# A gated cross-attention and expert layer on one Trainium2 core: the last norm's root on two engines, the clip flag in registers, the heads in another order

## The reference

```python
x = x + tanh(g_xattn[0]) * xattn(layernorm(x), ctx_768, Wq, bq, Wk, bk, Wv, bv, Wo, bo)
x = x + tanh(g_ffn[0]) * ffn(layernorm(x), gate_weight, w1, b1, w2, b2)
# layernorm: (x - mean) / sqrt(var + 1e-5), over the last axis
# xattn: 8 batches, 512 queries of width 256, 512 keys of width 192, 16 heads of 16
attn = clip(q @ k.T * 16 ** -0.5, -10000, 10000)
attn = softmax(attn)
attn = where(any(isnan(attn)), 1 / 512, attn)
out = (attn @ v) @ Wo + bo
# ffn: 8 experts of 1024 hidden units over all 4096 tokens
logits = x @ gate_weight.T
gates = logits * (logits >= the 6144th smallest logit)
y = sum over experts e of gates[:, e] * (gelu(x @ w1[e].T + b1[e]) @ w2[e].T + b2[e])
```

## Time and profile before

| | us |
|---|---|
| three executions | 1980.11, 1981.48, 1983.56 (median 1981.48) |
| profiled execution | 1980.04 |
| its span | 1978.2 |
| TensorE busy | 1891.1 (96%) |
| VectorE busy | 1323.6 (67%) |
| ScalarE busy | 1241.2 (63%) |
| GpSimd busy | 147.0 (7%) |
| TensorE's granted clock over the span | 0.979 of full |

### The profile page before, as it was taken

One profiled execution on the slowest core, in us unless ns is written; L12 is line 12 of the kernel. 1 busy time (PEld: TensorE's weight loads), 2 busy tenths in 40 slices (PEclk: granted clock), 3 DMA queues, 4 the chain that ended last, 5 costly groups with the idle time before them and its releaser, 6 DMA issues.

```text
span 1978.2 us, 26040 instructions
## 1 busy us (share of the span) xinstructions
PE 1891.1 (96%) x8916; PEld 1356.8 (69%) x8916; DVE 1323.6 (67%) x2331; ACT 1241.2 (63%) x2081; POOL 147.0 (7%) x330
## 2 busy tenths in 40 slices
PE   6989999999968999999999999999999999999998
PEld 5743333333336877788788888878878888887886
DVE  6688888888734798565655665565665566656555
ACT  4447776776742323676766766667676676767665
POOL 4300111101112250000000000000000000000000
PEclk9979999999978999999999999999999999999999
DMA  7943323222110154433323333223422224232221
GB/s 239 332 124 87 87 69 83 72 72 73 50 54 24 75 187 178 154 117 112 107 85 123 144 116 108 86 107 128 144 92 106 107 91 164 102 112 85 107 107 54
DMA packets 97243, 220.81 MB, mean 112 GB/s; under 512 B 31314, under 2 KB 49492, under 8 KB 87892
## 3 DMA queue, kind: packets, MB, share of 16 engines
q1 hardware_dynamic: 97108, 219.12, 32.4%
HBM read 178.57 MB, written 40.24 MB: 111 GB/s over the span
## 4 chain that ended last, share of the span: by engine, by line
PE 66%; DVE 2%; ACT 1%; issue 1%; POOL 0%; ACTq 0%; DVEq 0%; POOLq 0%
PE ps_y L2152 31%; PE ps_h L2099 27%; PE ps_h L2059 4%; PE ps_y L2071 4%; DVE h_hi L2410 0%; ACT gelu L2313 0%; DVE h_lo L2414 0%; DVE early L2554 0%; DVE gated L2483 0%; DVE out_T_acc L2490 0%; ACT h_hi L2316 0%; ACT w_pair L2283 0%; DVE candidate L2452 0%; DVE w_pair L2539 0%; DVE gate L2471 0%
## 5 line engine op out<-in xcount | busy, mean ns | idle before, releaser
L2414 DVE TENSOR_TENSOR h_lo<-gelu,h_hi 128x512 fp32r<-128x512 f32 x512 | 357.3, 702 | 406.3 <-ACT h_hi L2316 405.2
L2099 PE MATMUL ps_h<-x_hi,w_pair 128*128 128x512 f32 x1568 | 566.7, 395 | 1.4 <-ACT gelu L2313 1.0
L2313 ACT ACTIVATE gelu<-early,b 128x512 f32<-128x512 f32 x336 | 243.1, 724 | 228.4 <-DVE early L2554 220.9
L2099 PEld LDWEIGHTS ps_h<-x_hi,w_pair 128*128 128x128 f32 x1568 | 294.5, 188 | 77.1 <-issue 5.5
L964 DVE TENSOR_REDUCE low<-ps_s 128x1 f32<-128x512 f32 x512 | 322.2, 684 | 32.9 <-PE ps_s L820 29.5
L2316 ACT ACTIVATE h_hi<-gelu 128x512 fp32r<-128x512 f32 x448 | 283.3, 632 | 42.0 <-ACT gelu L2313 0.7
L2099 PE MATMUL ps_h<-x_lo,w_pair 128*128 128x512 f32 x784 | 308.8, 394 | 0.0
L1096 ACT ACTIVATE probs_T<-ps_t 128x512 f32<-128x512 f32 x384 | 207.8, 601 | 102.8 <-PE ps_t L830 101.1
L2554 DVE TENSOR_TENSOR early<-ps_h,copy 128x512 f32<-128x512 f32 x336 | 230.5, 686 | 51.1 <-PE ps_h L2099 51.1
L820 PE MATMUL ps_s<-k_st,q_st 48*128 48x512 f32 x512 | 204.0, 477 | 3.2 <-SPq L736 2.0
L2152 PE MATMUL ps_y<-h_hi,w_lo 128*128 128x512 f32 x512 | 203.0, 396 | 0.0
(11 more groups left out here) (252 smaller groups left out, 2611.4 us busy)
## 6 DMA issues: line engine op xcount, KB each, us to landing
x_hi<-blocks_scratch SPq DMA_DIRECT2D x28, 1024.0 KB, 5.1
x_lo<-blocks_scratch SPq DMA_DIRECT2D x28, 1024.0 KB, 8.8
x_hi<-blocks_scratch SPq DMA_DIRECT2D x28, 768.0 KB, 6.8
x_lo<-blocks_scratch SPq DMA_DIRECT2D x28, 768.0 KB, 10.2
gate<-gates_scratch SPq DMA_DIRECT2D x64, 256.0 KB, 3.2
q_st<-q_scratch SPq DMA_DIRECT2D x192, 64.0 KB, 2.4
k_st<-k_scratch SPq DMA_DIRECT2D x192, 64.0 KB, 2.3
k_scratch<-k_hl SPq DMA_DIRECT2D x8, 1024.0 KB, 3.9
```

Source lines behind the costliest of these rows:

```text
L2099: mm = pe.matmul(bank, w[wp], x[xp], start=start and n == 0, stop=n == 2, skip_group_check=not start)
L2313: act.activation(gelu[:, c % GELUS, :], src, ACT.Gelu_apprx_tanh, bias=b1[p][:, j:j + 1]).then_inc(gelu_done, 1)
L2414: dve.tensor_tensor(h_lo[:, j % RING, :], gelu[:, j % GELUS, :], h_hi[:, j % RING, :].bitcast(F32), ALU.subtract).then_inc(h_ready, 1)
```

## The change

Three edits, and bookkeeping for them.

- **Root.** For the last batch alone, GpSimd no longer makes the root. `last_root` on VectorE makes mean and variance, ScalarE takes one square root (`last_deviation`), and VectorE takes the reciprocal and a correction step. ScalarE takes a square root of a zero (`sqrt_ready`) earlier, behind its last weight split.
- **Flag.** Each engine reads the clip flag once, at the end of its list in `build_attend` and behind a semaphore, and keeps it in a register. The three later reads of it go, and the NaN flag's read and test move inside an outer `If(clip > 0)`.
- **Heads.** T takes the heads 0, 2, 1, 3 and S the heads 1, 3, 0, 2. In the first half of a step T has the upper rows and S the lower ones, in the second half the other way round.

```diff
-SCORE_HEADS = (1, 0, 3, 2)
+SCORE_HEADS = (1, 3, 0, 2)
+TURNED_HEADS = (0, 2, 1, 3)
...
+        def load_flag(name, eng):
+
+            eng.wait_ge(fits_summed, 2)
+            keep["clip"][name] = eng.value_load(keep["clip_flag"][0:1, 0:1], min_val=0, max_val=1)
...
-            with pool.Fori(0, BATCH) as b:
-
+            def bias(b):
...
+            with pool.Fori(0, BATCH - 1) as b:
+                bias(b)
                 reciprocal_root(b)
+            bias(BATCH - 1)
+            load_flag("pool", pool)
...
-            def scores_T(b, g, k, j, turn):
-
-                at = (g * TT + k) * GROUP + j
-                if k == 0 and j == 0:
+            def scores_T(b, g, k, i, turn):
+
+                at = (g * TT + k) * GROUP + i
+                j = TURNED_HEADS[i]
+                if k == 0 and i == 0:
...
+            def last_root():
+
+                mean, dev, diff, square, spread, var, root, root_2, scaled, rstd = (moments[:, i, :] for i in range(10))
+                first = (BATCH - 1) * 9
+                dve.wait_ge(stats_done, BATCH * 2)
+                dve.tensor_tensor(diff, stats[:, :, 1], stats[:, :, 4], ALU.subtract)
+                dve.tensor_tensor(dev, stats[:, :, 2], stats[:, :, 5], ALU.add)
+                dve.tensor_tensor(root, stats[:, :, 1], stats[:, :, 4], ALU.add).then_inc(moment_done, 1)
+                dve.wait_ge(moment_done, first + 1)
+                dve.scalar_tensor_tensor(out=square, in0=diff, scalar=0.25, in1=diff, op0=ALU.mult, op1=ALU.mult)
+                dve.tensor_scalar(spread, dev, 1.0 / DIM, EPS, ALU.mult, ALU.add)
+                dve.tensor_scalar(mean, root, 0.5, None, ALU.mult).then_inc(moment_done, 1)
+                dve.wait_ge(moment_done, first + 2)
+                dve.tensor_tensor(var, spread, square, ALU.add).then_inc(moment_done, 1)
+                dve.wait_ge(moment_done, first + 4)
+                dve.reciprocal(root, scaled).then_inc(moment_done, 1)
+                dve.wait_ge(moment_done, first + 5)
+                dve.tensor_tensor(root_2, root, root, ALU.mult).then_inc(moment_done, 1)
+                dve.wait_ge(moment_done, first + 6)
+                dve.scalar_tensor_tensor(out=diff, in0=root_2, scalar=-0.5, in1=var, op0=ALU.mult, op1=ALU.mult).then_inc(moment_done, 1)
+                dve.wait_ge(moment_done, first + 7)
+                dve.scalar_tensor_tensor(out=rstd, in0=diff, scalar=1.5, in1=root, op0=ALU.add, op1=ALU.mult).then_inc(rstd_done, 1)
+
             def layer_norm(b, i):
+                if b == BATCH - 1 and i == 0:
+                    last_root()
...
-                dve.tensor_scalar(keep["clip_flag"][:], ps_t[0][:, 0:1], 3 * HEADS * TOKENS - 0.5, None, ALU.is_lt)
+                dve.tensor_scalar(keep["clip_flag"][:], ps_t[0][:, 0:1], 3 * HEADS * TOKENS - 0.5, None, ALU.is_lt).then_inc(fits_summed, 1)
...
-                for j in heads:
-                    act.wait_ge(t_in_psum, n * GROUP + j + 1)
-                    act.activation(probs_T[k][:, j, :], ps_t[bank_of(turn, (g * TT + k) * GROUP + j)][:], ACT.Exp, scale=-1.0).then_inc(exp_done, 1)
+                for i in places:
+                    act.wait_ge(t_in_psum, n * GROUP + i + 1)
+                    act.activation(probs_T[k][:, TURNED_HEADS[i], :], ps_t[bank_of(turn, (g * TT + k) * GROUP + i)][:], ACT.Exp, scale=-1.0).then_inc(exp_done, 1)
...
+            def last_deviation():
+
+                act.wait_ge(moment_done, (BATCH - 1) * 9 + 3)
+                act.activation(moments[:, 8, :], moments[:, 5, :], ACT.Sqrt).then_inc(moment_done, 1)
...
                         if b == BATCH and (g, k) == (0, TT - 1):
                             first_high(1, w2_raw)
+                            act.activation(sqrt_ready[:], zero[:, 0:1], ACT.Sqrt)
+                        if b == BATCH and (g, k) == (1, TT - 1):
+                            last_deviation()
...
+            load_flag("act", act)
...
-            clip = pe.value_load(keep["clip_flag"][0:1, 0:1], min_val=0, max_val=1)
+            clip = keep["clip"]["pe"]
             with pe.If(clip > 0):
...
-            uniform = pe.value_load(keep["nan_flag"][0:1, 0:1], min_val=0, max_val=1)
-            with pe.If(uniform > 0):
+            clip = keep["clip"]["pe"]
+            with pe.If(clip > 0):
+                uniform = pe.value_load(keep["nan_flag"][0:1, 0:1], min_val=0, max_val=1)
+                with pe.If(uniform > 0):
```

More of the change, by code:

```diff
@@ L1577, in _ @@
         def _(sp):
[L1578 to L1586, removed]
-                    sp.dma_start(x_res[:], io["x"][bass.ds(b * SEQ, SEQ), :].rearrange("(t p) d -> p t d", p=P)).then_inc(batch_loaded, 16)
-                    sp.wait_ge(added, b + 1)
-                    sp.dma_start(scratch["x2"][bass.ds(b * SEQ, SEQ), :].rearrange("(t p) d -> p t d", p=P), x_res[:]).then_inc(x2_stored, 16)
-                batch(0)
-                with sp.Fori(1, BATCH) as b:
-                    batch(b)
-                sp.wait_ge(x2_stored, 16 * BATCH)
+            clip = keep["clip"]["sp"]
@@ new lines, in _, with batch @@
+            with sp.If(clip > 0):
+                uniform = sp.value_load(keep["nan_flag"][0:1, 0:1], min_val=0, max_val=1)
+                with sp.If(uniform > 0):
+                    sp.dma_start(wo[:], io["Wo"].rearrange("(k p) n -> p k n", p=P)).then_inc(consts_ready, 16)
+                    sp.dma_start(bo[:], io["bo"].rearrange("(a n) -> a n", a=1).to_broadcast([P, DIM])).then_inc(consts_ready, 16)
+                    def batch(b):
+                        wait(sp, x2_stored, b * 16)
+                        src = scratch["v"][bass.ds(b, 1), :, :].rearrange("a p (n w) -> (a p) n w", w=VW)
+                        sp.dma_start(v[:].rearrange("p t (h d) -> p (t h) d", d=HDIM), src[:, :, 0:HDIM]).then_inc(batch_loaded, 16)
+                        sp.dma_start(x_res[:], io["x"][bass.ds(b * SEQ, SEQ), :].rearrange("(t p) d -> p t d", p=P)).then_inc(batch_loaded, 16)
+                        sp.wait_ge(added, b + 1)
+                        sp.dma_start(scratch["x2"][bass.ds(b * SEQ, SEQ), :].rearrange("(t p) d -> p t d", p=P), x_res[:]).then_inc(x2_stored, 16)
+                    batch(0)
+                    with sp.Fori(1, BATCH) as b:
+                        batch(b)
+                    sp.wait_ge(x2_stored, 16 * BATCH)
@@ L1596, in _ @@
         @block.gpsimd
         def _(pool):
-            uniform = pool.value_load(keep["nan_flag"][0:1, 0:1], min_val=0, max_val=1)
-            with pool.If(uniform > 0):
-                pool.memset(share[:], 1.0 / SEQ).then_inc(consts_ready, 1)
+            clip = keep["clip"]["pool"]
+            with pool.If(clip > 0):
+                uniform = pool.value_load(keep["nan_flag"][0:1, 0:1], min_val=0, max_val=1)
+                with pool.If(uniform > 0):
+                    pool.memset(share[:], 1.0 / SEQ).then_inc(consts_ready, 1)
@@ new lines, in _ @@
+            with pe.If(clip > 0):
+                uniform = pe.value_load(keep["nan_flag"][0:1, 0:1], min_val=0, max_val=1)
+                with pe.If(uniform > 0):
+                    pe.wait_ge(consts_ready, 33)
+                    with pe.Fori(0, BATCH) as b:
+                        pe.wait_ge(batch_loaded, b * 32 + 32)
+                        for k in range(KT):
+                            for t in range(TT):
+                                mm = pe.matmul(ps_mean[:, k, :], v[:, t, k * P:(k + 1) * P], share[:],
+                                               start=(t == 0), stop=(t == TT - 1))
+                        mm.then_inc(mean_in_psum, 1)
+                        pe.wait_ge(mean_ready, b + 1)
+                        for k in range(KT):
+                            mm = pe.matmul(ps_y[:], mean_T[:, k, :], wo[:, k, :], start=(k == 0), stop=(k == KT - 1))
+                        mm.then_inc(y_in_psum, 1)
@@ L1627, in _ @@
         @block.vector
         def _(dve):
[L1629 to L1640 removed]
+            clip = keep["clip"]["dve"]
@@ new lines, in _ @@
+            with dve.If(clip > 0):
+                uniform = dve.value_load(keep["nan_flag"][0:1, 0:1], min_val=0, max_val=1)
+                with dve.If(uniform > 0):
+                    dve.wait_ge(consts_ready, 33)
+                    with dve.Fori(0, BATCH) as b:
+                        dve.wait_ge(y_in_psum, b + 1)
+                        dve.tensor_tensor(y[:], ps_y[:], bo[:], ALU.add).then_inc(y_ready, 1)
+                        dve.wait_ge(batch_loaded, b * 32 + 32)
+                        dve.wait_ge(y_ready, b + 1)
+                        for t in range(TT):
+                            ins = dve.scalar_tensor_tensor(out=x_res[:, t, :], in0=y[:], scalar=keep["tanh_g"][:, 0:1], in1=x_res[:, t, :],
+                                                           op0=ALU.mult, op1=ALU.add)
+                        ins.then_inc(added, 1)
```

61 lines of the change are left out of this document (22 added, 39 removed).

## The result

The changed kernel takes 1973.49 us (median of 6 runs, 1972.51 to 1975.27), the kernel before, run beside it, 1983.14 (6 runs, 1980.11 to 1985.56). The ratio is 0.9949, 95% interval 0.9938 to 0.9959: faster by 0.51%, or 9.65 us between the medians. Forecast were 3.7. The profiled execution took 1972.75, span 1970.9.

The account below looks back on a forecast made before the run. TensorE was taken as the bound, chiefly in the experts' part, whose earlier start shortens the whole. Root 2.7 + flag 1.5 - heads 0.5 = 3.7 us off the median 1981.48 gave 1977.8 us; range 1974.9 to 1981.0.

Parts of the forecast that it names:

- Root: Last norm's root, between attention and experts: normalising starts 1.84 us behind the statistics instead of 4.61; 2.7 us gained.
- Flag: Clip flag reads at the block ends before the experts: three removed, one added at attention's end; 1.5 us gained.
- Pages: Rival, chance 0.20: experts' code arrives at a fixed time behind the first jump, so the flag gains only 0.2 us.
- Halves: Rival, chance 0.07: in attention, loading weights into a streaming half costs time, 26 us over 120 steps; median 2003.
- Clock behind the root: Rival, chance 0.08: shorter root gap may keep TensorE at 2.4 GHz, some 2.3 us more; 6.0 gained, median 1975.5.
- Last batch: Last two groups of the last batch: lone T pairs share a half; -0.5 us, with 0 and -2.5 as ends.
- Cost in the steady batches 0: Attention's steady batches: the new head order runs the same pairs on two halves, so nothing gained or lost.
- my signs of being wrong: Forecast is wrong if the steady batch moves from 56.0 us, or the root's chain takes over 2.6 us.

Follow-up runs that it names:

- e5: Changed kernel with the old T order 0, 1, 2, 3 in groups 2 and 3 of the last batch: 1974.46 us, ratio 0.9947.
- e1: Kernel before with the two new orders of heads alone, root and flag as before: 1979.80 us, ratio 0.9978.
- e7: Changed kernel with the new head orders only in groups 3 and 0, round the turn of a batch: 1973.15 us, ratio 0.9945.
- e8: Changed kernel with the new head orders only in groups 1 and 2, old ones round the turn: 1979.50 us, ratio 0.9970.
- e9: Changed kernel with the S order made equal to the T order, so each pair needs the same half of TensorE: 2096.73 us, ratio 1.0573.
- e10: Changed kernel with old head orders and one T product computed twice just ahead of each turn and one just behind: 1976.83 us, ratio 0.9965.
- l7: Second profile of the kernel with old head orders and two more T products round each turn; profiled execution 1976.09 us.

## Why the prediction was wrong, point by point

- **Root**: 2.7 forecast, 2.64 measured. The chain took 1.97, 0.13 more than summed: links of 0.20 rather than 0.18, the reciprocal's 0.21. The table load ran at 572.6 and cost nothing.
- **Flag**: 1.5 forecast, 1.44 measured. VectorE's read stands behind the logits, the other engines' earlier.
- **Pages** (0.20): did not occur here. The third jump on TensorE stayed at 0.208.
- **Halves** (0.07, slower): no cost. The batch is 55.97.
- **Clock behind the root** (0.08): no. TensorE's gap was down to 3.07 us (578.60 to 581.67), and its clock still went to 0.50 at 581.9, for 20.5 us.
- **Last batch**: -0.5 forecast, -0.49 measured. That is partly luck, for e5 gave back only 0.24 of it where I had put all.
- **"Cost in the steady batches 0"**: this step failed. It is right of a batch at full clock and wrong of the kernel, for the change took away the stretches of half clock behind the turns, 2.4 to 2.8 us each. Each of the four profiles of before has one, so some 2.6; by whole times e1 measured some 4, and e7 against e8, which differ in the order alone, 6.4 (by their medians). I had that stretch before me in the earlier trace rows, wrote that it comes and goes with the clock, and asked of the new order only what it does to the start of each product. None of my signs of being wrong would have caught it: the full-clock batch stayed at 56.0 and the root's chain under 2.6.

One term is thus missing in the sum, 2.6 by the traces and 4 to 6 by whole times. The time, 1973.49, is 4.3 below the forecast and 1.4 below the range. The gain is 6.0 above the forecast, since the kernel before, too, came out 1.7 above the median that I started from.

**What stays open.** Why the order of the halves acts on the clock; the runs show only that it does, and where. Also, with parts of the change alone the times moved more than the traces account for (root 5.5 by ratio against 2.6; flag 3.2 against 1.3), and the three parts by themselves add up to 0.66% where the whole has 0.51%, and the kernel before's mean of 65, 1984.0, is 2.5 above that of its four profiled executions. None of its profiles is of an execution above 1983, so what those have more is not shown.

## What to carry to other kernels

A batch that is 5% longer than its twins at a granted clock of 0.94 is a row to explain, not to subtract: find where the stretch begins, and ask of each part of a change what TensorE will be doing just there. An order of products that leaves a batch at full clock as long as it was can still be worth as much as the steps that you can add up. And when two profiles differ in such a stretch, count it over several before you believe either.

## What the runs showed that I had not expected

**The clock falls in dense work.** It fell behind a turn after 3 us with TensorE busy 2.79, and in e9 after 3 us with TensorE busy without a gap. The profile's busy columns are no forecast of the granted clock; the windows' PEclk column has to be read by itself.

**What the rival with the pages named, a third jump that grows, came one kernel further.** e10 puts 16 more products into TensorE's code, and TensorE's jump over the clipped version of the experts' block grew. That line in e10:

```profile
L2079 PEldq COMPARE_BRANCH  x1: 1826/1826/1826, 600.4 to 600.4; - x1
```

And in its second profile, l7:

```profile
L2079 PEldq COMPARE_BRANCH  x1: 1741/1741/1741, 597.5 to 597.5; - x1
```

In the kernel after it is 208. From the logits to the first product these two took 8.58 and 8.50 instead of 6.67 and 6.82, so all that the flag gained was gone again, with the reads still out. The Trainium skill, "Runtime: NRT & Kernel Launch", section "Instruction fetch mechanics", says that a branch to outside the resident pages forces a fetch; e10 agrees with it in kind, at some 1.6 us here, while the first jump takes 3.3 to 3.9 in all the kernels. That the fetch is the cause is argued and not shown: the runs show that the jump grew with the added products and at no other change. That a jump costs 0.2 in one version says nothing about the next.
